# A gated cross-attention and mixture-of-experts block on one core: each batch's x loaded ahead into the rows that later hold its normalised x, scatters placed round the last norm, and the routing weights of all batches made in one go

## The chip, the core and the metric

The program runs on one core of a Trainium2 chip. The metric is the device time of one execution in microseconds (us). Before the change the median of 3 runs is 420.44 us (420.35 to 422.11). A difference under 0.5% (2.1 us) is about what a measurement of this kernel cannot tell from no change.

## The reference, cut to what matters

Eight batches (NB = 8) of 100 tokens (SQ = 100) with 512 features (H = 512), each with a context of 722 rows. First a cross-attention with one head whose output is tiled 16 times, with scores normalised along the keys before the softmax; then a mixture of 8 experts of which each token takes two.

```python
def _L0_xattn_ref(query, key, value, mask, Wq, bq, Wk, bk, Wv, bv, Wout, bout, seq_mask):
    q = query @ Wq + bq
    k = key @ Wk + bk
    v = value @ Wv + bv
    scores = jnp.einsum('bqd,bkd->bqk', q, k) / math.sqrt(HIDDEN)
    scores = _layer_norm_scores(scores)
    scores = scores + jnp.where(m, jnp.float32(-1e-32), jnp.float32(0.0))
    attn = jax.nn.softmax(scores, axis=-1)
    head = jnp.einsum('bqk,bkd->bqd', attn, v)
    attention = jnp.tile(head, (1, 1, NUM_HEADS))
    return attention @ Wout + bout

def _L0_ffn_ref(x, router_w, w13, w2):
    logits = jnp.einsum('bsh,eh->bse', x, router_w)
    probs = jax.nn.softmax(logits, axis=-1)
    weights, indices = jax.lax.top_k(probs, K)
    weights = weights / (weights.sum(axis=-1, keepdims=True) + 1e-06)
    h13 = jnp.einsum('bsh,ehi->bsei', x, w13)
    gate, up = jnp.split(h13, 2, axis=-1)
    h = jax.nn.silu(gate) * up
    y = jnp.einsum('bsei,eih->bseh', h, w2)
    y_sel = jnp.take_along_axis(y, indices[..., None], axis=2)
    return (y_sel * weights[..., None]).sum(axis=2)
x = x + jnp.tanh(g_xattn[0]) * _L0_xattn_ref(_layernorm(x, axis=-1), ctx_1024, ...)
x = x + jnp.tanh(g_ffn[0]) * _L0_ffn_ref(_layernorm(x, axis=-1), ...)
```

## The kernel before, in words

The program is written out by hand for each engine, with semaphores between them; no scheduler moves anything. It has two stages.

**Attention, in rounds.** Round i (from -1 to 7) works on several batches at once. PE (lines 413 to 432) projects batch i's context to keys and values (L319), turns the probabilities of batch i-1 (L330), makes the query of batch i+1 (L305), turns the values and makes the scores of batch i (L338, L344), makes the head of i-1 (L356), the ranks of i-2 (L363, L364) and the output rows of i-1 (L372). DVE (lines 840 to 864) takes in turn `choose(i-2)` (the two best experts of each token), `add_attention(i-2)` (x plus the attention, and the statistics of the second norm), `make_weights(i-3)`, `ln1_stats(i+2)` (statistics of the raw x), `fix_query(i+1)`, `make_values(i)`, `score_stats(i)`, `make_places(i-2)`, `set_pick(i-2)`, `raw_logits(i-1)`. POOL (lines 1033 to 1045) takes `count_taken(i-2)`, `norm2(i-2)`, `mark_sums(i)`, `norm1(i+2)`, `sigma(i)` (the factor and bias of the softmax of batch i, on which ACT's exponential L532 waits), and `scatter(i-3)`: two indirect DMAs (L1014) that write each token of a batch into the lists of its two experts in DRAM. ACT makes the exponentials, the copies out of PSUM, stores x plus attention to the output (`store_x2`, L561), and writes the normalised rows into `xn2[:, b, :]` (`normalise2`, L554), which it also puts into DRAM (L557). SP loads x, the transposed x and the context of the batches in their order, then the first expert's weights (L244, L281).

The raw x of batch b lies in `x_t[b % 6]`, a ring of six places of which two are the tiles yw and xg. `add_attention` writes its sum over it in place, so the load of batch 6 has to wait for the norm and the store of batch 0, and that of batch 7 for those of batch 1. These waits stand in SP's own order, ahead of everything that it loads later:

```python
                if b >= NX:
                    sp.wait_ge(S["xn2_ready"], b - NX + 1)
                    sp.wait_ge(S[f"out_put{b % NX}"], 16 * (b // NX))
                load_x(b)
```

**Between the stages.** After the last round PE picks the rows of the first tile by matmuls with `pick` (L380), which need the normalised rows of all batches; POOL works off what is left (`norm2` of batches 6 and 7 and the last scatters); DVE makes the tables of tiles. ACT copies the first tile's rows (`first_x_hi`, L634), DVE their low part (L943), and PE starts tile 0.

**Experts, in tiles of 128 list entries.** There are 16 tiles. Weights come as 1 MB pieces; ACT makes the high part of each piece (`split_hi`, L600, units 0 to 9 for one expert) and DVE the low part (`split_lo`, L819). For tile t PE does the gate and up products (L473), turns h (L480), turns the x rows of the next tile (`turn_x`, L460) and does the down products (L493); ACT makes silu (L644) and the scaled output rows (`y_out`, L660). In the last tile of each expert ACT and DVE also split the weights of the next expert. Behind `y_out` on ACT stand the split of units 8 and 9 and the next tile's silu. POOL runs a serial chain: `fetch(t+1)` (the piece of the list, L1080; the indices, L1082; the gather of the rows, L1086; the gather of the weights, L1092), `add_rows(t-1)` (the scatter-add into the output, L1106, whose landing it waits for), `entries_pass(t)` (L1101, for which `y_out(t)` waits). The loop is entered at `entries_stay(1)` (L1097). Ahead of it POOL waits for all scatters to land, starts the list of tile 0 (L1112), does `fetch(1)`, and gathers the weights of tile 0 (L1117). SP starts the next expert's loads (L289, L293; 6 MB) when the gather of `fetch(1)` has landed.

## Time and profile before

| what | us |
|---|---|
| median of 3 runs | 420.44 |
| the profiled execution, its own time | 422.71 |
| its span, first to last instruction | 421.1 |
| PE busy / DVE / ACT / POOL | 377.9 / 224.4 / 190.1 / 165.6 |
| mean granted clock of PE, as a share of 2.4 GHz | 0.952 |
| DMA: 77.75 MB | mean 185 GB/s |

The span is the time between the first and the last instruction of one profiled execution; the execution's own time is 1.6 us longer. Busy time adds up all instructions of an engine; an engine can be idle with no harm done. The places in the span are us from its start. In what follows T0 is the start of tile 0's first matmul.

### The profile page before, as it was taken

What the parts mean: (1) busy time and instruction counts of PE and PEld (TensorE: products, weight loads), DVE (VectorE), ACT (ScalarE), POOL (GpSimd) and SP (SyncE); (2) the same over time, 40 slices, a digit from 0 to 9 for tenths busy, and PEclk for the clock granted to TensorE, in tenths of its full rate; (3) what the DMA queues carried; (4) which work ended last, traced back from release to release, by engine and by line L of the source; (5) the groups of instructions that cost most, each with busy time, mean ns of one, the idle gap of its engine ahead of it and who ended that gap; (6) DMA issues with size and microseconds to landing.
All of it is one profiled execution on the core that took longest, in us unless ns stands there. A gap on an engine that the chain in (4) does not pass through costs nothing.

```text
span 421.1 us, 7238 instructions
## 1 busy us (share of the span) xinstructions
PE 377.9 (90%) x2046; PEld 288.2 (68%) x2047; DVE 224.4 (53%) x470; ACT 190.1 (45%) x314; POOL 165.6 (39%) x259
## 2 busy tenths in 40 slices
PE   1979994996868999998999999999999999999970
PEld 1435553475657887886888888888888888888850
DVE  2135883697930765387862239618644762973110
ACT  1123452464711862468642246528625643852220
POOL 2433574578941405515132241613434151451310
PEclk9979996899797999999999999999999999999995
DMA  7976799721208988197982228726762982210301
GB/s 253 372 258 199 273 326 352 292 80 48 33 5 309 418 341 246 28 313 271 371 307 42 50 48 291 237 102 186 262 232 33 324 252 82 50 27 4 50 0 16
DMA packets 18828, 77.75 MB, mean 185 GB/s; under 512 B 4957, under 2 KB 6109, under 8 KB 11647
## 3 DMA queue, kind: packets, MB, share of 16 engines
q1 hardware_dynamic: 11870, 66.80, 44.0%
q0 software_dynamic: 5184, 7.52, 9.5%
q10 hardware_dynamic: 1760, 3.28, 2.5%
q8 instruction: 6, 0.10, 0.1%
q14 instruction: 8, 0.06, 0.1%
HBM read 70.95 MB, written 7.55 MB: 186 GB/s over the span
## 4 chain that ended last, share of the span: by engine, by line
PE 66%; DMA 16%; POOL 6%; issue 6%; ACT 2%; DVE 1%; POOLq 1%; DVEq 0%; SPq 0%; ACTq 0%
PE scp L493 18%; PE turnB L473 17%; PE turnA L473 16%; PE kvp L319 4%; DMA x_t<-in_x_dram 3%; PE kvp L480 3%; DMA lists_d<-entry,place 3%; DMA ent_next<-lists_d 2%; DMA out_dram<-yw,ent 2%; DMA mask_u<-in_mask_dram 2%; POOL lists_d L1014 2%; PE scp L460 2%; DMA xg<-xn_d,gidx 1%; PE scp L344 1%; PE turnA L372 1%
## 5 line engine op out<-in xcount | busy, mean ns | idle before, releaser
L819 DVE TENSOR_TENSOR w13l<-stage,w13h 128x1024 fp32r<-128x1024 f32 x64 | 76.0, 1219 | 4.0 <-ACT w13h L600 3.4
L600 ACT ACTIVATE w13h<-stage 128x1024 fp32r<-128x1024 f32 x64 | 65.0, 1053 | 0.0
L473 PE MATMUL turnA<-w13h,xTh 128*128 128x512 f32 x128 | 51.8, 405 | 1.6 <-DVE xTl L943 1.6
L493 PE MATMUL scp<-w2h,hTh 128*128 128x512 f32 x128 | 52.2, 407 | 0.0
L473 PE MATMUL turnB<-w13h,xTh 128*128 128x512 f32 x128 | 52.0, 406 | 0.0
L473 PE MATMUL turnA<-w13h,xTl 128*128 128x512 f32 x128 | 51.4, 402 | 0.0
L473 PE MATMUL turnA<-w13l,xTh 128*128 128x512 f32 x128 | 51.4, 401 | 0.0
L473 PE MATMUL turnB<-w13l,xTh 128*128 128x512 f32 x128 | 50.9, 398 | 0.0
L493 PE MATMUL scp<-w2h,hTl 128*128 128x512 f32 x128 | 50.7, 396 | 0.0
L473 PE MATMUL turnB<-w13h,xTl 128*128 128x512 f32 x128 | 50.6, 395 | 0.0
L493 PE MATMUL scp<-w2l,hTh 128*128 128x512 f32 x128 | 50.5, 394 | 0.0
L819 DVE TENSOR_TENSOR w2l<-stage,w2h 128x2048 fp32r<-128x2048 f32 x16 | 35.9, 2288 | 21.3 <-ACT w2h L600 21.3
L913 DVE TENSOR_TENSOR h_t<-turnA,sg 128x256 f32<-128x256 f32 x32 | 12.8, 420 | 55.4 <-ACT sg L644 54.9
L1106 POOL DMA_INDIRECT out_dram<-yw,ent x16 | 29.8, 1862 | 15.8 <-ACT yw L660 11.3
L660 ACT ACTIVATE yw<-scp,ent 128x512 f32<-128x512 f32 x16 | 11.0, 687 | 51.1 <-PE scp L493 48.4
L644 ACT ACTIVATE sg<-turnB 128x256 f32<-128x256 f32 x32 | 12.3, 384 | 47.3 <-PE turnB L473 47.3
L1101 POOL COPY ent<-ent_now 128x3 int32<-128x3 int32 x15 | 4.8, 323 | 71.3 <-DMA out_dram<-yw,ent 71.3
L913 DVE TENSOR_TENSOR h_t<-turnB,sg 128x256 f32<-128x256 f32 x32 | 13.5, 422 | 34.0 <-ACT sg L644 29.4
L1014 POOL DMA_INDIRECT lists_d<-entry,place x16 | 27.9, 1744 | 6.1 <-issue 5.8
L473 PEld LDWEIGHTS turnA<-w13h,xTh 128*128 128x128 f32 x128 | 24.6, 192 | 7.7 <-issue 1.9
L917 DVE TENSOR_TENSOR hTl<-kvp,hTh 128x256 fp32r<-128x256 f32 x64 | 24.0, 416 | 10.9 <-ACT hTh L649 10.6
L600 ACT ACTIVATE w2h<-stage 128x2048 fp32r<-128x2048 f32 x16 | 29.7, 1904 | 0.0
(177 smaller groups left out, 654.3 us busy)
## 6 DMA issues: line engine op xcount, KB each, us to landing
stage<-in_w_dram SPq DMA_DIRECT2D x48, 1024.0 KB, 6.6
ctx_t<-in_ctx_dram SPq DMA_DIRECT2D x8, 1444.0 KB, 12.1
xT_t<-in_xT_dram SPq DMA_DIRECT2D x8, 200.0 KB, 8.2
xn_d<-xn ACTq DMA_DIRECT2D x8, 200.0 KB
x_t<-in_x_dram SPq DMA_DIRECT2D x6, 200.0 KB
out_dram<-x_t ACTq DMA_DIRECT2D x6, 200.0 KB
stage<-in_wout_dram SPq DMA_DIRECT2D x1, 1024.0 KB, 12.3
lists_d<-entry,place POOLq DMA_INDIRECT x16, 5.3
```

What stands on the lines that cost most here:

```text
L319: mm = pe.matmul(kvp[strip * D:(strip + 1) * D, 0:HK], sm[:, o:o + D], ctx_t[b % NC][:, c, half * HK:(half + 1) * HK], start=(c == 0), sto ...
L473: mm = pe.matmul(region, xp[:, c, :], wp[:, q, c, :], start=(c == 0 and i == 0), stop=(c == HC - 1 and i == 2))
L480: mm = pe.transpose(kvp[:, (q % 2) * 512 + j * P:(q % 2) * 512 + (j + 1) * P], h_t[:, q, j * P:(j + 1) * P], ident[:])
L493: mm = pe.matmul(scp[:, 512:512 + H], hp[:, q, j * P:(j + 1) * P], wp[:, q * QC + j, :], start=(q == 0 and j == 0 and i == 0), stop=(q == ...
L600: act.activation(dst, src, ACT.Copy).then_inc(S["w_hi"], 1)
L644: act.activation(sg[q % 2][:], region, ACT.Silu).then_inc(S["silu_done"], 1)
L660: act.activation(yw[:], scp[:, 512:512 + H], ACT.Copy, scale=ent[:, 2:3].bitcast(F32)).then_inc(S["y_ready"], 1)
L819: dve.tensor_tensor(lo, raw, hi.bitcast(F32), ALU.subtract).then_inc(S["w_lo"], 1)
L913: dve.tensor_tensor(h_t[:, q, :], region, sg[q % 2][:], ALU.mult).then_inc(S["h_done"], 1)
L917: dve.tensor_tensor(hTl[:, q, :], kvp[:, (q % 2) * 512:(q % 2) * 512 + QW], hTh[:, q, :].bitcast(F32), ALU.subtract).then_inc(S["hl_done"], 1)
L1014: pool.indirect_dma_start(lists_d, bass.IndirectOffsetOnAxis(place[:, b, k:k + 1], 0), entry[:, b, k, :], None).then_inc(S[f"lists_put{k}" ...
L1106: pool.indirect_dma_start(out_rows, bass.IndirectOffsetOnAxis(ent[:, 0:1], 0), yw[:], None, bounds_check=T - 1, oob_is_err=False, compute_ ...
```

## The change

It has five parts.

1. x of batch b is loaded into `xn2[:, b, :]`, the place of its normalised rows (eight places, so no load waits for a buffer). In SP's order the loads of x stand one batch earlier, and the waits for the norm, the store and `wx9_made` are gone. `add_attention` writes its sum into a ring `x2` of four (yw, xg and two more), and waits there for the store and the norm of batch b-4.
2. `scatter(b)` goes in round b+2, a round earlier. After the rounds POOL takes norm2(6), scatter(6), norm2(7), scatter(7); before, the scatters of batches 5, 6 and 7 were all still to do.
3. `make_weights` runs once for all eight batches, behind the low part of the first tile's x; `logit_exp` keeps its results by batch and no longer waits for it.
4. On DVE the low splits of units 0 and 1 stand in rounds 6 and 7, those of 2 and 3 after `add_attention(6)` (before: unit 0 in round 7, 1 and 2 after `add_attention(6)`, 3 after the tables). Ahead of unit 4 DVE waits for `lists_sent`, which POOL gives once its last scatter is issued.
5. POOL waits for the lists, the tables and the store, does `fetch(1)` first, and only then starts the list of tile 0.

```diff
-        NC, NX, NT = 3, 6, 3
+        NC, NX, NT, N2 = 3, NB, 3, 4
-        x_t = [sb(a, f"x_t{i}", [SQ, H])[:] for i in range(NX - 2)] + [yw[0:SQ, :], xg[0:SQ, :]]
+        x2 = [yw[0:SQ, :], xg[0:SQ, :]] + [sb(a, f"x2{i}", [SQ, H])[:] for i in range(N2 - 2)]
...
-                sp.dma_start(x_t[b % NX], x[b]).then_inc(S[f"x_in{b % NX}"], 16)
+                sp.dma_start(xn2[:, b, :], x[b]).then_inc(S[f"x_in{b % NX}"], 16)
...
+            load_x(3)
             load_ctx(2)
...
             for b in range(3, NB):
-                if b == 4:
-                    sp.wait_ge(S["wx9_made"], 1)
-                if b >= NX:
-                    sp.wait_ge(S["xn2_ready"], b - NX + 1)
-                    sp.wait_ge(S[f"out_put{b % NX}"], 16 * (b // NX))
-                load_x(b)
+                if b + 1 < NB:
+                    load_x(b + 1)
...
-            sp.wait_ge(S["weight_made"], NB)
+            sp.wait_ge(S["weight_made"], 1)
...
             def logit_exp(b):
                 act.wait_ge(S["nlmax_done"], b + 1)
-                if b >= 1:
-                    act.wait_ge(S["weight_made"], b)
...
             def add_attention(b):
                 dve.wait_ge(S["out_done"], b + 1)
-                dve.scalar_tensor_tensor(out=x_t[b % NX], in0=outp[0:SQ, :], scalar=gs[:, 0:1], in1=x_t[b % NX],
+                if b >= N2:
+                    dve.wait_ge(S[f"out_put{b % N2}"], 16 * (b // N2))
+                    dve.wait_ge(S["xn2_ready"], b - N2 + 1)
+                dve.scalar_tensor_tensor(out=x2[b % N2], in0=outp[0:SQ, :], scalar=gs[:, 0:1], in1=xn2[:, b, :],
...
-                if live(i - 3):
-                    make_weights(i - 3)
-                if i == NB - 1:
-                    split_lo(0, 0)
+                if i >= NB - 2:
+                    split_lo(0, i - NB + 2)
...
-            make_weights(NB - 3)
-            for unit in (1, 2):
+            for unit in (2, 3):
                 split_lo(0, unit)
...
-            make_weights(NB - 1)
+            make_weights()
+            dve.wait_ge(S["lists_sent"], 1)
             for unit in range(4, W_UNITS):
                 split_lo(0, unit)
...
-            for i in ROUNDS:
-                if live(i - 2) and i <= NB:
+            for i in range(-1, NB):
+                if live(i - 2):
                     count_taken(i - 2)
-                if live(i - 2):
                     norm2(i - 2)
...
-                if live(i - 3):
-                    scatter(i - 3)
+                if live(i - 2):
+                    scatter(i - 2)
...
-            for k in range(2):
-                pool.wait_ge(S[f"lists_put{k}"], 16 * NB)
+            count_taken(NB - 2)
+            norm2(NB - 2)
+            scatter(NB - 2)
+            norm2(NB - 1)
+            scatter(NB - 1)
+            pool.sem_inc(S["lists_sent"], 1)
...
+            for k in range(2):
+                pool.wait_ge(S[f"lists_put{k}"], 16 * NB)
+            pool.wait_ge(S["tiles_ready"], 1)
+            pool.wait_ge(S["out_put1"], 32)
+            fetch(1)
             pool.dma_start(ent[:, 0:2], lists_d[0:P, :]).then_inc(S["first_in"], 16)
-            pool.wait_ge(S["tiles_ready"], 1)
-            pool.wait_ge(S["out_put5"], 16)
-            fetch(1)
```

SP's order of loads round batches 5 to 7 (x_t, xT_t and ctx_t are x, the transposed x and the context of a batch; stage is a 1 MB piece of the first expert's weights), before:

```order
L235 DMA xg<-in_x_dram 100x512
L238 DMA xT_t<-in_xT_dram 128x400
L241 DMA ctx_t<-in_ctx_dram 128x2888
L244 DMA stage<-in_w_dram 128x2048
L235 DMA x_t<-in_x_dram 100x512
L238 DMA xT_t<-in_xT_dram 128x400
L241 DMA ctx_t<-in_ctx_dram 128x2888
L244 DMA stage<-in_w_dram 128x2048
L235 DMA x_t<-in_x_dram 100x512
L238 DMA xT_t<-in_xT_dram 128x400
L241 DMA ctx_t<-in_ctx_dram 128x2888
```

and in the changed kernel, the same stretch:

```order
L235 DMA xn<-in_x_dram 100x512
L238 DMA xT_t<-in_xT_dram 128x400
L241 DMA ctx_t<-in_ctx_dram 128x2888
L244 DMA stage<-in_w_dram 128x2048
L235 DMA xn<-in_x_dram 100x512
L238 DMA xT_t<-in_xT_dram 128x400
L241 DMA ctx_t<-in_ctx_dram 128x2888
L244 DMA stage<-in_w_dram 128x2048
L238 DMA xT_t<-in_xT_dram 128x400
L241 DMA ctx_t<-in_ctx_dram 128x2888
```

The x ahead of a batch's transposed x is now that of the next batch, so the last group has none, and x(7) stands ahead of batch 6's context instead of behind it.

POOL's order after the last softmax factor (L1002 before, L997 now), through the norms (L988 to L993; now L983 to L988) and the scatters (L1014; now L1009) to the fetch for tile 1, before:

```order
L1002 TENSOR_SCALAR sig<-lns,sig 100x1
L1014 DMA lists_d<-entry,place 7296x2 x2
L1007 TENSOR_TENSOR taken<-taken,both 100x8
...
L993 TENSOR_SCALAR rs<-ltop,rs 100x1
L1014 DMA lists_d<-entry,place 7296x2 x2
L988 TENSOR_SCALAR ve<-ln 100x1
...
L993 TENSOR_SCALAR rs<-ltop,rs 100x1
L1014 DMA lists_d<-entry,place 7296x2 x4
L1112 DMA ent<-lists_d 128x2
```

and now:

```order
L997 TENSOR_SCALAR sig<-lns,sig 100x1
L1009 DMA lists_d<-entry,place 7296x2 x2
L1002 TENSOR_TENSOR taken<-taken,both 100x8
...
L988 TENSOR_SCALAR rs<-ltop,rs 100x1
L1009 DMA lists_d<-entry,place 7296x2 x2
L983 TENSOR_SCALAR ve<-ln 100x1
...
L988 TENSOR_SCALAR rs<-ltop,rs 100x1
L1009 DMA lists_d<-entry,place 7296x2 x2
L1077 TENSOR_LOAD tile_row
```

Two scatters of the eight that followed the last factor have gone into the rounds, and the list of tile 0 (L1112) no longer stands ahead of the fetch.

## Rows read from the trace of the kernel before

**Rows 1.** Windows: us; busy of PE, PEld, DVE, ACT, POOL; clock, DMA share, GB/s.
```profile
52.48:59.80 7.32, 7.32 (x76) 4.11 (x75) 6.44 (x29) 3.93 (x8) 5.71 (x13) 1.00 0.99 359
59.80:74.64 14.84, 9.38 (x76) 5.17 (x75) 7.25 (x34) 6.02 (x12) 8.11 (x19) 0.75 0.99 332
74.64:83.27 8.63, 8.63 (x76) 4.41 (x75) 5.04 (x21) 3.74 (x7) 3.86 (x10) 0.84 0.79 289
91.33:107.11 15.78, 10.73 (x94) 8.85 (x92) 11.52 (x47) 9.20 (x15) 12.96 (x16) 0.92 0.20 53
134.35:152.40 18.05, 18.05 (x85) 14.76 (x84) 12.88 (x17) 11.74 (x18) 5.22 (x4) 1.00 1.02 402
```
**Rows 2.** Chain that ended last, in order of time: start, us, what.
```profile
54.42 14.53 DMA x_t<-in_x_dram
...
107.45 11.18 DMA lists_d<-entry,place
...
166.38 0.66 PE scp L460 x4
```
**Rows 3.** SP's timeline: a weight piece, x(6), context 7.
```profile
40.89 0.43 SPq L244 DMA_DIRECT2D stage<-in_w_dram  x1
...
51.51 0.31 SPq L235 DMA_DIRECT2D x_t<-in_x_dram  x1
...
55.17 0.43 SPq L241 DMA_DIRECT2D ctx_t<-in_ctx_dram  x1
```
**Rows 4.** PE's timeline, the two long stops.
```profile
70.42 1.27 PE L356 MATMUL turnA<-probT,vn 128*64 128x100 f32 x12 [5.41 <-DVE vn L738]
...
127.81 1.11 PE L460 MATMUL scp<-ident,xg 128*128 128x128 f32 x4 [4.99 <-DMA xg<-xn_d,gidx]
```
**Rows 5.** POOL's timeline, one round with scatters.
```profile
56.74 0.21 POOL L1007 TENSOR_TENSOR taken<-taken,both 100x8 f32<-100x8 f32 x1
...
58.75 0.23 POOL L979 TENSOR_SCALAR ve<-ln 100x1 f32<-100x1 f32 x1
...
61.18 0.27 POOL L1002 TENSOR_SCALAR sig<-lns,sig 100x1 f32<-100x1 f32 x1
...
64.41 0.21 POOL L1007 TENSOR_TENSOR taken<-taken,both 100x8 f32<-100x8 f32 x1
```
**Rows 6.** DVE's timeline, low splits ahead of and in tile 0.
```profile
93.15 2.35 DVE L819 TENSOR_TENSOR w13l<-stage,w13h 128x1024 fp32r<-128x1024 f32 x2
...
101.69 1.21 DVE L819 TENSOR_TENSOR w13l<-stage,w13h 128x1024 fp32r<-128x1024 f32 x1
...
107.56 4.62 DVE L819 TENSOR_TENSOR w13l<-stage,w13h 128x1024 fp32r<-128x1024 f32 x4
112.11 4.49 DVE L819 TENSOR_TENSOR w2l<-stage,w2h 128x2048 fp32r<-128x2048 f32 x2
```
**Rows 7.** POOL's timeline beside them, and into the expert stage.
```profile
93.28 3.08 POOL L1014 DMA_INDIRECT lists_d<-entry,place  x1 [0.30 <-issue]
...
101.93 1.11 POOL L991 TENSOR_SCALAR rs<-ln,rs 100x1 f32<-100x1 f32 x1
...
107.45 10.01 POOL L1014 DMA_INDIRECT lists_d<-entry,place  x1 [0.30 <-issue]
...
124.36 1.09 POOL L1086 DMA_INDIRECT xg<-xn_d,gidx  x1 [0.85 <-POOL gidx L1082]
...
127.01 0.95 POOL L1117 DMA_INDIRECT ent<-weights_d,ent  x1 [0.30 <-issue]
130.57 0.18 POOL L1097 COPY ent_now<-ent_next 128x3 int32<-128x3 int32 x1 [2.61 <-issue]
```
**Rows 8.** ACT's timeline, the high splits ahead of the last norm.
```profile
99.60 2.93 ACT L600 ACTIVATE w13h<-stage 128x1024 fp32r<-128x1024 f32 x3
```
**Rows 9.** Line L241, the eight loads of context: from issue to landing.
```profile
DMA to landing us min/median/max: 6.2/12.1/17.9
```
**Rows 10.** Line L1092, the sixteen gathers of weights: from issue to landing.
```profile
DMA to landing us min/median/max: 2.5/3.2/7.5
```

More of the change, by code:

```diff
@@ L160, in gated_block @@
         taken = sb(a, "taken", [SQ, NB + 1, E])
[L161 removed]
+        wgt = sb(a, "wgt", [SQ, 3, NB])
         hr = sb(a, "hr", [SQ, 2, E])
@@ L179, in gated_block @@
         xTl = sb(es, "xTl", [P, HC, P], F32R)
[L182 to L183 removed]
+        names = """x_in0 x_in1 x_in2 x_in3 x_in4 x_in5 x_in6 x_in7 xT_in0 xT_in1 xT_in2 ctx_in0 ctx_in1 ctx_in2 small_in wout_in bout_in mask_in
+        lists_set lists_put0 lists_put1 out_put0 out_put1 out_put2 out_put3 xn2_put weights_put lists_sent
         ident_made ones_made inv_made sel_made zero_made iotas_made empty_made mask_made emask_made tanh_done
@@ L553, in normalise2 @@
                 act.wait_ge(S["nmean2"], b + 1)
-                act.activation(xn2[:, b, :], x_t[b % NX], ACT.Identity, bias=rs2[b % 2][:, 1:2], scale=rs2[b % 2][:, 0:1]
+                act.activation(xn2[:, b, :], x2[b % N2], ACT.Identity, bias=rs2[b % 2][:, 1:2], scale=rs2[b % 2][:, 0:1]
                                ).then_inc(S["xn2_ready"], 1)
@@ L801, in set_pick, with make_weights @@
                                          op0=ALU.is_equal, op1=ALU.mult).then_inc(S["pick_set"], 1)
-            def make_weights(b):
-                dve.wait_ge(S["lexp_done"], b + 1)
-                dve.tensor_tensor(wgt[:, 0:1], e8[:, 0:1], e8[:, 1:2], ALU.add).then_inc(S["wgt_sum"], 1)
-                dve.wait_ge(S["wgt_sum"], b + 1)
-                dve.scalar_tensor_tensor(out=wgt[:, 1:2], in0=e8s[:], scalar=TOPK_EPS, in1=wgt[:, 0:1],
-                                         op0=ALU.mult, op1=ALU.add).then_inc(S["wgt_eps"], 1)
-                dve.wait_ge(S["wgt_eps"], b + 1)
-                dve.reciprocal(wgt[:, 2:3], wgt[:, 1:2]).then_inc(S["wgt_rec"], 1)
-                dve.wait_ge(S["wgt_rec"], b + 1)
-                dve.tensor_scalar(wt[:, b, :], e8[:, 0:2], wgt[:, 2:3], g_t[0:SQ, 1:2], ALU.mult, ALU.mult
-                                  ).then_inc(S["weight_made"], 1)
+            def make_weights():
+                dve.wait_ge(S["lexp_done"], NB)
+                dve.tensor_tensor(wgt[:, 0, :], e8[:, :, 0], e8[:, :, 1], ALU.add).then_inc(S["wgt_sum"], 1)
+                dve.wait_ge(S["wgt_sum"], 1)
+                dve.scalar_tensor_tensor(out=wgt[:, 1, :], in0=e8s[:], scalar=TOPK_EPS, in1=wgt[:, 0, :],
+                                         op0=ALU.mult, op1=ALU.add).then_inc(S["wgt_eps"], 1)
+                dve.wait_ge(S["wgt_eps"], 1)
+                dve.reciprocal(wgt[:, 2, :], wgt[:, 1, :]).then_inc(S["wgt_rec"], 1)
+                dve.wait_ge(S["wgt_rec"], 1)
+                dve.scalar_tensor_tensor(out=wt[:], in0=e8[:, :, 0:2], scalar=g_t[0:SQ, 1:2],
+                                         in1=wgt[:, 2, :].unsqueeze(2).to_broadcast([SQ, NB, 2]),
+                                         op0=ALU.mult, op1=ALU.mult).then_inc(S["weight_made"], 1)
             def split_lo(e, unit):
@@ L879, in _ @@
             dve.tensor_scalar(fill[:], steps_num[:], count, None, ALU.is_lt, ALU.add, accum_out=nt[:, 1:2]).then_inc(S["nt_ready"], 1)
-            make_weights(NB - 2)
             dve.wait_ge(S["nt_ready"], 1)
@@ L1119, in _ @@
             pool.sem_inc(S["ent_copied"], 1)
-            for j in range(NX):
-                pool.wait_ge(S[f"out_put{j}"], 16 * ((NB - 1 - j) // NX + 1))
+            for j in range(N2):
+                pool.wait_ge(S[f"out_put{j}"], 16 * NB // N2)
             n_tiles = pool.value_load(first_tile[0:1, E:E + 1], min_val=E, max_val=TILES - 1)
```

18 lines of the change are left out of this document (7 added, 11 removed).

## The prediction

> **What bounds the kernel now.** I read the windows by stage first, then the chain that ended last, then the timelines of PE, SP, POOL and DVE where the chain leaves PE. The reader is to see three things.
>
> First, a steady attention round takes 7.32 us with PE busy throughout, but the next two take 14.84 and 8.63 [rows 1], 8.8 us too much. In the first of them PE stands for 5.41 us at L356 behind DVE's values [rows 4], and DVE stands there because `ln1_stats(7)` is ahead in its order and x(7) has not landed: it is issued at 54.42 and lands 14.53 us later [rows 2]. It is late because SP was held before x(6) until 51.51 [rows 3] by the store of batch 0. The rest of the 8.8 is clock: 0.75 and 0.84 granted instead of 1.00 in these two windows [rows 1].
>
> Second, from the last softmax factor (91.33) to the first matmul of tile 0 (T0, 107.11) there are 15.78 us [rows 1].
>
> Third, the expert stage's first two tiles are bound by POOL's serial chain, not by PE. The chain goes from the last scatter (107.45, with its landing 11.18 us) through the fetches to the gather of x(3), which PE turns at 166.38 [rows 2]. From T0, a PE that never stood would be there after 15.5 us (its stop before 127.81 of 4.99 us begins at 122.8, somewhat over T0 + 15.5 [rows 4]) and two tiles of 18.05 [rows 1]: at T0 + 51.6 = 158.7. So 7.7 us of the end come from POOL's chain, and shortening PE's stop alone gives nothing. 
> *Loads of x ahead.* x(6) and x(7) now depend on no store. x(7) goes right behind the weight piece of 40.89 [rows 3], x(6) earlier; even at 17.9 us, the longest that a context takes [rows 9], it is there at 59.2, ahead of PE's stop, which begins at 65.0 (70.42 - 5.41 [rows 4]). The stop and its low clock go. Late next is POOL. Its own round with scatters takes 64.41 - 56.74 = 7.67 us [rows 5], above PE's 7.32, and the scatters now begin a round earlier. Before, sigma(4) is ready at 61.45; one POOL-bound round more makes that 61.8 (7.67 - 7.32). Another at 7.67 gives 69.5 for sigma(5). The next has no `norm1` (two of the six instructions from 58.75 to 61.45 [rows 5], 0.9 us of the 2.7), so 6.8 gives 76.3; the last is PE's again, 7.25: 83.5. The low splits of units 0 and 1 now stand in rounds 6 and 7. By where they fall, one misses POOL's reads narrowly and one holds a scatter for about half a microsecond, partly in slack: 0.2. sigma(7) is ready at 83.7 instead of 91.33: **-7.6**. Bounds: if each of the two splits holds POOL for its 1.2 us [rows 6] with some 0.4 for what follows, -4.5; if neither does, -7.8.
>
> *DVE's ring of four and the batched weights.* The store of b-4 is issued four rounds before its place is written, over 20 us; a landing is at most some 18 us in the fullest stretch. 28 small instructions of `make_weights` go, but DVE has idle time in every round, and the 0.85 us of the remaining run stands where one batch's stood. 0.
>
> *Context 7.* Issued at 55.17 [rows 3], it landed at worst 17.9 us later [rows 9], 73.1. PE will want it at 75.2 (59.80 and two rounds of 7.67) instead of 83.27. Less is queued ahead of it than before. 0, with 2 us of cover; if that is gone, each microsecond costs one.
>
> *The tail of the attention.* Two scatters less stand ahead of T0, but on T0's path it is these that count: the 3.08 us scatter (2.1 too long) meets its split otherwise; the split of unit 3 no longer stretches the last norm (0.84) but, waiting for ACT, meets norm2(6) and costs about 1.0. POOL would be ready 1.9 us sooner, but ACT's three high splits of 2.93 us [rows 8] end only 10.1 us behind sigma(7) (now 102.53, 11.2 behind; they follow norm2(6), which comes 1.1 sooner), and there the last normalisation then starts, instead of 11.7 behind, when L991 was done (103.04 [rows 7]): **-1.6**. Bounds 0 and -1.9. T0 becomes 83.7 + 14.2 = 97.9.
>
> *From T0 to POOL's loop.* Before, the loop begins at 130.57 [rows 7], T0 + 23.5. Now the scatters are issued by T0 - 0.9, ahead of the splits, so `lists_sent` holds DVE for nothing, and the lists land by T0 + 2.5. The list for tile 1 follows at T0 + 6. But its index instruction L1082 falls into the run of splits, which ends at T0 + 9.5 as before: the block moves from the scatter to the fetch. The gather is then issued at T0 + 10.4, lands 3.45 us later (127.81 - 124.36 [rows 4, 7]), ahead of PE's need at T0 + 15.5; the stop of 4.99 us goes. Behind the gather come the weights, and only now the list of tile 0, issued at 13.1, and its weights at 15.6. Before, L1117 at 127.01 stood 9.5 us behind the scatter's end; now it is 6.1 behind the end of the splits. But SP's 6 MB start when the gather lands, T0 + 14, and these two transfers run into them. A gather of weights takes 2.5 to 7.5 us to land [rows 10]; I take 5, between the median and the longest, as traffic is dense. With 1.3 us of register work the loop starts at T0 + 22: **-1.5** beside T0's own gain. Bounds: 2.5 us landings give T0 + 19.4 (-4.1); 7.5 and a late list T0 + 26.5 (+3.0).
>
> *From the loop to x(3).* 130.57 to 166.38 is 35.8 us of serial transfers in weight traffic; the same traffic follows the same engines, so I take the same 35.8. PE now reaches x(2) ahead of it and stops there for 3 to 4 us, a stop that before lay in tile 0; the clock falls behind such a stop (the window with a 5.41 us stop shows 0.75 [rows 1]). I add **+0.5**, for most of it is hidden in POOL's chain. Bounds 0 and 2. Tile 3 on is PE's and unchanged.
>
> Sum: -7.6 - 1.6 - 1.5 + 0.5 = **-10.2 us**. It is made against the profiled execution of 422.71 us, which would be 412.5; the median of the runs is 2.3 us lower, so 420.44 - 10.2 = **410.2**.
>
> **Rule against row.** The last scatter stood for the whole run of six splits, 10.01 us. The Trainium skill, page "SBUF — State Buffer", section "SBUF: two separate sides", holds that whichever of a DVE and a GpSimd operation starts first has the shared ports for that one instruction. By it the waiting read would get in at the next boundary of two splits, after 1.2 us at most; the trace disagrees before, but it is a rival here (below). The same page, section "Who interferes with whom", infers that a tensor_tensor on DVE does not stop descriptor generation on GpSimd; were that so, the 10.01 us would belong to the scatter, which is the slower rival.
>
> **Rivals.** *(a) The fetch gets in between the splits.* Its read could fall on a boundary where a split waits for ACT. Then the gather goes at T0 + 7 instead of 10.4 and everything behind it is 3 to 4 us earlier: 410.2 - 4 = 406. Against it the unbroken 10.01 us. 0.12.
>
> *(b) Context 7 takes the place of x(7).* DMA share is 0.99 already [rows 1], and the rounds want the data 8 us sooner. Landing 7 us after the need costs 5 net: 415. For it the 17.9 us; against it that it would need 24. 0.12.
>
> *(c) The first entries are late.* The list and weights of tile 0 land at the slow end, the loop starts at T0 + 26.5 and PE's stop in tile 1 grows: +4.5, 414.7, and with POOL held twice by the splits in the rounds (3 us) 417.7. 0.12.
>
> *(d) Slower: the long issue belongs to the scatters.* If it is the backlog of POOL's queue and not DVE's splits, the place of the block is open, and it can fall on scatter(6), which now stands ahead of norm2(7). Price: 9.0 us on T0 and, as DVE waits for `lists_sent`, another such issue of scatter(7), from T0 - 1.9 to T0 + 8.1, holds splits 4 to 9 by 7.5: 410.2 + 9.0 + 7.5 = 426.7. It decides once the block is over the 9.2 us of T0's gain. Against it: three long POOL instructions all end with DVE's splits, and one of them is no DMA. 0.03.
>
> *(e) Little is gained.* The rounds stay as they are because POOL, not x, sets them, and the fetch chain gives the rest back: within 2.1 us of 420.4. 7.67 against 14.84 speaks against it. 0.03.
>
> **How the numbers follow.** The forecast has 0.58, its own range by the bounds 406.5 to 414.5. To hold eight in ten I reach to (a), (b) and part of (c): 404.5 to 416.5. PE's floor for x(3), T0 + 51.6 = 149.5, is 6.4 us under POOL's chain (166.38 - 10.7 + 0.2 = 155.9), so nothing lies under 404. Faster by over 0.5% is the forecast, (a), (b) and most of (c): 0.94; same 0.03; slower 0.03.
>
> **What would show it.** Right: rounds of 7.3 to 7.7 us to the end and no stop at L356; sigma(7) near 84; T0 near 98; no scatter over 3 us; L1082 for tile 1 some 3 us long, ending with the sixth split; no PE stop before x(1), one of 3 to 4 us before x(2); L1097's first at T0 + 22. Wrong: a stop at the projection of batch 7, DVE idle before split 4, or an L1082 of 0.2 us.

## The result, and the profile after

The changed kernel takes **416.38 us** (median of 4 runs, 414.67 to 418.47) beside 421.27 us for the kernel before (4 runs, 420.35 to 423.28): ratio 0.989, 95% interval 0.984 to 0.994. It is faster, by 4.9 us, where 10.2 were forecast. Beside its own variants on two further chips there was no gain to be seen: 421.01 against 419.67 us (run e1, ratio 1.007 [1.002, 1.012]) and 418.52 against 419.49 us (run e10, 1.004 [0.999, 1.010]). So the 4.9 us hold for the first set of runs alone. The kernel before spreads over 412.6 to 428.0 us on the chips of the experiments (one run of 947.65 left aside), far more than the 2.1 us put down ahead for what cannot be told from no change. Each ratio is taken over the runs within 1.5% of the kernel's fastest, so it can differ from the quotient of the medians.

The profiled execution after takes 417.08 us (span 415.5), 5.6 less than the one before. Its windows by stage answer to [rows 1] (columns as there: us; busy of PE, PEld, DVE, ACT, POOL; granted clock, DMA share, GB/s):

```profile
59.89:67.56 7.67, 7.38 (x75) 4.13 (x74) 5.76 (x25) 4.89 (x9) 6.09 (x15) 1.00 1.01 341
67.56:75.22 7.66, 7.39 (x75) 4.13 (x74) 6.14 (x24) 4.88 (x9) 5.96 (x15) 1.00 1.00 328
75.22:83.55 8.33, 7.67 (x76) 4.62 (x76) 6.71 (x28) 5.06 (x10) 6.81 (x14) 1.00 0.66 217
83.55:100.10 16.55, 12.97 (x98) 10.90 (x96) 9.57 (x39) 9.36 (x15) 10.20 (x15) 0.79 0.28 84
100.10:115.13 15.03, 15.03 (x63) 12.11 (x63) 11.48 (x14) 7.32 (x12) 7.96 (x6) 0.89 0.12 25
115.13:138.05 22.92, 18.22 (x87) 14.68 (x85) 11.47 (x17) 11.41 (x19) 6.72 (x7) 0.99 1.00 402
138.05:158.19 20.14, 19.58 (x85) 15.81 (x85) 10.06 (x12) 8.48 (x13) 7.12 (x7) 0.93 0.67 217
...
176.29:198.02 21.73, 19.82 (x86) 15.87 (x85) 17.18 (x20) 15.03 (x21) 7.95 (x8) 0.92 0.84 302
198.02:216.80 18.78, 18.20 (x87) 14.70 (x85) 11.19 (x16) 9.14 (x15) 7.99 (x7) 1.00 0.80 289
```

The round of 14.84 us is gone; the rounds are 7.67 and 7.66, and the last softmax factor (sigma(7)) is ready at 83.55 instead of 91.33. But from there to T0 it now takes 16.55 us, not 15.78, at a clock of 0.79. And the tile from 176.29 to 198.02 takes 21.73 us.

SP's timeline shows x(7) and context 7, for [rows 3]:

```profile
40.85 0.37 SPq L235 DMA_DIRECT2D xn<-in_x_dram  x1
...
54.66 0.33 SPq L241 DMA_DIRECT2D ctx_t<-in_ctx_dram  x1
```

PE's timeline, the tail and the stops in the tiles, for [rows 4] (the last bracket is the idle time before the group and what ended it):

```profile
90.92 0.34 PE L360 MATMUL turnB<-both,tri 100*100 100x8 f32 x2 [1.30 <-issue]
...
91.54 2.45 PE L377 MATMUL kvp<-pick,xn 100*128 100x128 f32 x16
94.11 2.08 PE L377 MATMUL kvp<-pick,xn 100*128 100x128 f32 x8
96.27 2.08 PE L377 MATMUL kvp<-pick,xn 100*128 100x128 f32 x8
100.10 0.79 PE L470 MATMUL turnA<-w13h,xTh 128*128 128x512 f32 x1 [1.75 <-DVE xTl L937]
...
138.05 0.69 PE L457 MATMUL scp<-ident,xg 128*128 128x128 f32 x2 [4.70 <-DMA xg<-xn_d,gidx]
...
191.59 0.43 PE L477 MATMUL kvp<-ident,h_t 128*128 128x128 f32 x2 [1.91 <-DVE h_t L907]
```

DVE's timeline in the tail (splits of units 2 and 3, then the last batch's choice), which answers to [rows 6]:

```profile
85.02 1.19 DVE L818 TENSOR_TENSOR w13l<-stage,w13h 128x1024 fp32r<-128x1024 f32 x1
87.78 1.23 DVE L818 TENSOR_TENSOR w13l<-stage,w13h 128x1024 fp32r<-128x1024 f32 x1 [1.57 <-ACT w13h L595]
...
90.70 0.17 DVE L772 TENSOR_TENSOR both<-hot 100x8 f32<-100x8 f32 x1
```

Read the two together. Unit 3's low split stands 1.57 us for ScalarE's high split. Behind it on DVE wait the last batch's places, logits and `both`; PE needs `both` at L360 and stands 1.30 us (its row says issue, but `both` ends at 90.87 and PE starts at 90.92; the same stop in e13 below names it). The clock then falls, 16 picks run partly slow, and the two groups of eight take 2.08 us each at a granted clock of 0.50, where they take 1.16 at full clock. That is how T0 comes to 100.10.

POOL's timeline, for [rows 7]:

```profile
77.94 1.81 POOL L1009 DMA_INDIRECT lists_d<-entry,place  x1 [0.30 <-issue]
...
95.84 0.99 POOL L1009 DMA_INDIRECT lists_d<-entry,place  x1 [0.30 <-issue]
...
104.92 4.61 POOL L1080 TENSOR_SCALAR gidx<-ent_next 128x1 int32<-128x1 int32 x1 [3.55 <-DMA ent_next<-lists_d]
...
115.05 1.00 POOL L1117 DMA_INDIRECT ent<-weights_d,ent  x1 [1.70 <-DMA ent<-lists_d]
122.07 0.18 POOL L1095 COPY ent_now<-ent_next 128x3 int32<-128x3 int32 x1 [6.03 <-issue]
```

The 10.01 us scatter is gone. In its place the index instruction of tile 1 stands 4.61 us under DVE's splits (100.41 to 109.44), and POOL's loop starts at 122.07, T0 + 21.97. x(3) is turned at 158.19 instead of 166.38.

### The profile page after: what moved, and what is told of

It is laid out like the page before. It is cut to its first block, busy times and chain, and to the rows that moved or that the text cites. A ratio compares the mean times of both kernels' runs of the same rounds, so it can differ in the third digit from the quotient of the medians.

```text
span 415.5 us, 7206 instructions
## 1 busy us (share of the span) xinstructions
PE 376.4 (91%) x2046; PEld 288.1 (69%) x2047; DVE 220.7 (53%) x442; ACT 190.4 (46%) x314; POOL 164.2 (40%) x259
## 4 chain that ended last, share of the span: by engine, by line
PE 62%; DMA 18%; issue 7%; POOL 6%; DVE 2%; POOLq 2%; ACT 1%; DVEq 0%
PE scp L490 14%; PE turnB L470 14%; PE turnA L470 14%; DMA out_dram<-yw,ent 7%; PE kvp L316 6%; DMA ent_next<-lists_d 6%; PE turnA L302 2%; PE kvp L477 2%; DMA xg<-xn_d,gidx 2%; POOL gidx L1080 2%; PE turnA L369 2%; POOL ent_next L1090 1%; DMA ent<-weights_d,ent 1%; PE scp L457 1%; PE turnA L353 1%
## 5 line engine op out<-in xcount | busy, mean ns | idle before, releaser
L1104 POOL DMA_INDIRECT out_dram<-yw,ent x16 | 31.5, 1972 | 15.6 <-ACT yw L655 11.0
L1099 POOL COPY ent<-ent_now 128x3 int32<-128x3 int32 x15 | 6.8, 454 | 69.5 <-DMA out_dram<-yw,ent 69.5
L1084 POOL DMA_INDIRECT xg<-xn_d,gidx x16 | 25.1, 1571 | 13.4 <-POOL gidx L1080 13.4
```

The costliest lines, as they stand in the source:

```text
L1084: pool.indirect_dma_start(xg[:], None, xn2_d, bass.IndirectOffsetOnAxis(gidx[:], 0)).then_inc(S["gathered"], 16)
L1104: pool.indirect_dma_start(out_rows, bass.IndirectOffsetOnAxis(ent[:, 0:1], 0), yw[:], None, bounds_check=T - 1, oob_is_err=False, compute_ ...
```

## The experiments

16 runs of 12 kernels in five sets; the kernels of a set ran on one chip beside the kernel before. "Splits" are the low splits on DVE; "x ahead" is part 1 of the change.

| run | kernel | us, median (range) | before beside it | ratio, 95% interval |
|---|---|---|---|---|
| e1 | the whole change | 421.01 (419.72-422.30) | 419.67 | 1.007 [1.002, 1.012] |
| e2 | x ahead alone | 412.96 (408.46-417.41) | 419.67 | 0.979 [0.972, 0.986] |
| e3 | scatters, splits, fetch order; not x ahead | 418.65 (417.06-422.56) | 419.67 | 1.002 [0.997, 1.008] |
| e4 | whole, unit 3 late | 420.32 (419.08-422.50) | 419.67 | 1.006 [1.000, 1.011] |
| e5 | whole, units 0 to 3 at their old places | 412.58 (411.75-414.70) | 418.63 | 0.994 [0.990, 0.998] |
| e6 | whole, scatters at their old places | 419.89 (417.72-421.23) | 418.63 | 1.011 [1.003, 1.019] |
| e7 | e2, DVE holds back twice | 415.92 (414.16-419.17) | 418.63 | 1.001 [0.997, 1.006] |
| e8 | e2 again | 413.93 (408.12-418.72) | 418.63 | 0.983 [0.969, 0.997] |
| e9 | e5 again | 414.30 (412.37-416.05) | 419.49 | 0.994 [0.990, 0.998] |
| e10 | the whole change | 418.52 (415.53-422.08) | 419.49 | 1.004 [0.999, 1.010] |
| e11 | e5, list of tile 0 first | 409.30 (407.85-410.40) | 419.49 | 0.983 [0.977, 0.989] |
| e12 | e11, DVE waits for the index | 411.11 (409.48-413.89) | 419.49 | 0.988 [0.982, 0.995] |
| e13 | e5, unit 3 early | 417.67 (414.42-419.58) | 422.18 | 0.988 [0.984, 0.992] |
| e14 | e5, unit 0 in round 6 | 413.43 (412.95-414.14) | 422.18 | 0.980 [0.977, 0.983] |
| e15 | e14, list of tile 0 first | 408.27 (405.57-409.67) | 422.60 | 0.965 [0.960, 0.970] |
| e16 | e11 again | 410.03 (407.18-412.09) | 422.60 | 0.967 [0.961, 0.973] |

### e1 to e4: which part carries the gain

e1 is the kernel after, unchanged. e2 is the kernel before with every line of part 1 of the diff (`x_t` gone, `x2` a ring of four, x loaded into `xn2` a batch ahead), nothing else. e3 is the kernel before with parts 2, 4 and 5 alone, and its weights batch by batch. e4 is the whole change with

```diff
-            for unit in (2, 3):
-                split_lo(0, unit)
+            split_lo(0, 2)
...
                                      op0=ALU.mult, op1=ALU.add).then_inc(S["tiles_ready"], 1)
+            split_lo(0, 3)
```

> The changed kernel once more, as the measure for the others on this chip. Theory A (the lost microseconds sit at fixed places: T0 at 100.1 with the picks at the low clock, and one to two more behind a stop in tile 4): 414.5 to 417, T0 again at 100.1 with a granted clock of 0.5 between 94 and T0. Theory B (it was an unlucky draw of clock in one execution): T0 nearer 98 and the median under 413.

> Before plus part 1 alone (x loaded ahead, ring of four for the sums); scatters, splits, weights and the order of the fetch as before. Theory A (the load ahead is nearly all of the gain): the stop at L356 goes, sigma(7) at about 83, T0 = sigma(7) + 15.8 = 99, POOL's loop at T0 + 23.5 = 122.5, x(3) at 158.5, time as the whole change or within 1 us of it, 415 to 417. Rival (the scatters and the fetch carry half of it): 418 to 419.5.

> The change without part 1 and without the batched weights: x in the ring of six with SP's waits, scatters a round earlier, split positions, lists_sent and the fetch first as in the change. Theory A: the stop of some 5.4 us at L356 stays; the last scatter's issue is 1 us, L1080's index instruction is held for 4 to 5 us instead; T0 near 107, POOL's loop 1.5 us earlier than before, 419 to 421. Rival (the fetch order alone is worth its 4.99 us stop in tile 0): under 417.

> The changed kernel with one move: the low split of unit 3 again behind the tables of tiles, as before the change. Theory A (its new place makes DVE wait for ACT, so the ranks of batch 7 come late, PE stands 1.3 us, and the clock falls for the picks up to T0): DVE's wait of 1.6 us and PE's of 1.3 shrink to 0.7 or less, the clock from 91 to T0 is 1.0 up to the last norm, T0 at 98, and 2 us less than the changed kernel, 414. Rival (the picks run slow because they are few and small, wherever the split is): T0 stays at 100, no difference.

x ahead alone takes 412.96 us, 8 less than the whole change on the same chip. The rest of the change without it is worth nothing that could be told (418.65 against 419.67). So part 1 carries the whole gain and the other parts together give half of it or more back. Neither theory of e1 came out: 421.01 us lies above both ranges, with T0 at 104.09. e2 beat both of its ranges.

e3's forecast missed a thing that bears on the size of part 1. The stop at L356 was to stay at 5.4 us. In e3's profile it is 2.44 us (PE starts again at 59.72), and sigma(7) is ready at 87.71, where the one profile of the kernel before has 91.33. How long that stop is in other executions of the kernel before is not known, for it was profiled once. In this set sigma(7) is ready at 82.33 in e2, at 85.85 in e1 and at 87.71 in e3: with the other parts beside it, x ahead brings it 1.9 us forward here (e1 against e3).

Moving unit 3 alone (e4) did not bring the tail back: T0 was 104.44, beside 104.09 in e1. Both profiles have another fault, a stop of PE at L327 of 1.99 us, which the first profile of the change did not have. It is best seen in e10, the whole change on a third chip.

### e5, e6, e9, e10: splits or scatters

e5 and e9 are one kernel: scatters early, but the splits where they were before the change.

```diff
-                if i >= NB - 2:
-                    split_lo(0, i - NB + 2)
+                if i == NB - 1:
+                    split_lo(0, 0)
...
-            for unit in (2, 3):
+            for unit in (1, 2):
                 split_lo(0, unit)
...
+            split_lo(0, 3)
```

e6 keeps the splits of the change and puts the scatters back:

```diff
-                if live(i - 2):
-                    scatter(i - 2)
+                if live(i - 3):
+                    scatter(i - 3)
...
             norm2(NB - 2)
+            scatter(NB - 3)
+            norm2(NB - 1)
             scatter(NB - 2)
-            norm2(NB - 1)
             scatter(NB - 1)
```

> The whole change, but the low splits on VectorE stand where the kernel before has them (unit 0 in round 7, 1 and 2 behind add_attention(6), 3 behind the tables); the scatters stay a round early. Theory S (it is the splits in rounds 6 and 7, falling on POOL's reads, that make the tail late and low in clock): T0 is 97.5 to 99 instead of 100.1 to 104.1, no PE stop over 1 us after 80 us, time 411 to 414. Rival Q (it is POOL's queue with the scatters a round early, one pair more in front of each sigma): the rounds keep 7.7 to 7.9 us, T0 stays at 100 or later, 416 to 421.

> The whole change, but each scatter a round later again, as before the change; the splits stay in rounds 6 and 7. Theory S: T0 is late (100 to 104) as in the whole change, time 416 to 421, and some POOL instruction under a split takes 1 us more than its normal time. Rival Q: T0 98 to 99, rounds of 7.3 to 7.5 us, time 411 to 414.

> The whole change with the low splits at the places of the kernel before, once more, as the partner of the three others on this chip. Theory S: 411 to 415 again, T0 97.5 to 99.5, turns of x(2) and x(3) at T0+37 and T0+57, and 3 us or more under the whole change beside it.

> The whole change, a third time, beside its variants. Theory S: 415.5 to 421.5, T0 100 to 104, and its median at least 3 us over that of the variant with the splits at their old places; in its rounds 6 and 7 at least one POOL instruction is 1 us over its normal time under a split. If it comes out within 1 us of the variant, the placing of the splits is not what cost the gain.

The splits' places cost it. With them put back the kernel takes 412.58 and 414.30 us, 4.2 us under the whole change on the same chip (e9, e10); with the scatters put back instead it stays at 419.89. T0 is 98.35 and 97.30 in e5 and e9, 101.95 in e6, 100.30 in e10.

How they cost it: POOL's timeline of e10, a scatter in round 6, one in round 7, the last instruction of sigma(7),

```profile
69.11 2.20 POOL L1009 DMA_INDIRECT lists_d<-entry,place  x1 [0.52 <-issue]
...
76.91 2.12 POOL L1009 DMA_INDIRECT lists_d<-entry,place  x1 [0.53 <-issue]
...
83.83 1.36 POOL L997 TENSOR_SCALAR sig<-lns,sig 100x1 f32<-100x1 f32 x1
```

DVE's timeline of e10, the splits of units 0, 1, 2 and 3,

```profile
69.13 1.19 DVE L818 TENSOR_TENSOR w13l<-stage,w13h 128x1024 fp32r<-128x1024 f32 x1
...
76.85 1.19 DVE L818 TENSOR_TENSOR w13l<-stage,w13h 128x1024 fp32r<-128x1024 f32 x1
...
83.95 1.19 DVE L818 TENSOR_TENSOR w13l<-stage,w13h 128x1024 fp32r<-128x1024 f32 x1
...
88.65 1.23 DVE L818 TENSOR_TENSOR w13l<-stage,w13h 128x1024 fp32r<-128x1024 f32 x1 [3.51 <-ACT w13h L595]
```

and PE's timeline of e10:

```profile
86.23 0.73 PE L327 MATMUL turnB<-ident,prob 100*128 100x100 f32 x6 [1.99 <-ACT prob L529]
...
92.42 3.64 PE L377 MATMUL kvp<-pick,xn 100*128 100x128 f32 x16
```

Units 0 and 1 each begin together with a scatter, which takes 1.0 to 1.1 us over its normal 1.11. POOL bounds these rounds, so it stays late, and its last instruction of sigma(7) now meets unit 2's split and takes 1.36 us instead of 0.27. So sigma(7) is ready at 85.19 instead of 83.55, ScalarE's softmax is late, PE stands 1.99 us, and after that the 16 picks take 3.64 us (granted clock 0.53) where they took 2.05 in e5. In the first profile of the change the splits of units 0 and 1 began 0.6 and 1.2 us behind the first scatter of their round (70.04 against 69.47, 77.69 against 76.51), and held only the second, by 0.2 and 0.8 us: no stop. So it hangs on a fraction of a microsecond whether this placing stops PE at L327, and e1, e4, e6 and e10 all fell on the bad side, each with a stop of 1.99.

What the bad side costs is less regular. This table has, for each profile, when sigma(7) was ready, T0, the time between and the granted clock over it:

| run | unit 3 ahead | stop at L327 | sigma(7) | T0 | between | clock |
|---|---|---|---|---|---|---|
| after | yes | no | 83.55 | 100.10 | 16.55 | 0.79 |
| e13 (below) | yes | no | 85.29 | 101.81 | 16.52 | 0.96 |
| e10 | yes | yes | 85.19 | 100.30 | 15.11 | 0.89 |
| e6 | yes | yes | 85.29 | 101.95 | 16.66 | 0.69 |
| e1 | yes | yes | 85.85 | 104.09 | 18.24 | 0.54 |
| e4 | no | yes | 85.83 | 104.44 | 18.61 | 0.52 |
| e9 | no | no | 83.06 | 97.30 | 14.24 | 0.96 |
| e5 | no | no | 84.08 | 98.35 | 14.27 | 1.00 |
| e14 (below) | no | no | 83.33 | 97.58 | 14.25 | 1.00 |

e10 reaches T0 only 0.2 us behind the first profile, which was on the good side. e1 is the same kernel with the same stop and needs 3.1 us more than e10 behind sigma(7), at a clock of 0.54. What decides the clock there no run isolates, so the stop is shown and a fixed price for it is not. Of the 3.0 us by which e10's T0 lies behind e9's, 2.1 are ahead of sigma(7) and 0.9 behind it.

### e13, e14: which split

e13 puts unit 3 back to its place in the change, behind 1 and 2 (`for unit in (1, 2, 3)`, and none behind the tables); e14 puts unit 0 back into round 6 (`if i == NB - 2`).

> The scatters a round early, unit 0 in round 7 as before the change, and units 1, 2 and 3 together behind add_attention(6). If the split of unit 3 ahead of the last batch's values (where it waits for ScalarE, 3.5 us in the whole change) is what makes the tail late: T0 100 or later, DVE stands over 1.5 us before a split at 87 to 90, 416 to 419. If it is the split in round 6 and its twin in round 7 alone: no PE stop near 86, T0 98 to 99.5, 412 to 415.

> The scatters a round early, unit 0 in round 6 as in the whole change, units 1 and 2 behind add_attention(6) and 3 behind the tables as before the change. If the split in round 6 is enough to put POOL late: a scatter of 2.1 us near 69, sigma(7) ready at 84.5 to 85.5, a PE stop of 1 to 2 us near 86 and T0 at 99.5 to 104, 415 to 420. If it takes both splits (round 6 and round 7): sigma(7) ready at 83.5 to 84, T0 98 to 99, 412 to 415.

Unit 0 in round 6 alone did no harm: sigma(7) at 83.33, T0 at 97.58, 413.43 us. But its split began 0.56 us behind the scatter (69.77 against 69.21; 0.53 in e15), the good side of the first profile, so no run shows what it does alone on the bad side. With unit 3 early the kernel takes 4.2 us more (417.67), with no stop at L327 at all; the two also differ in unit 0's round. DVE's and PE's timelines of e13:

```profile
90.95 1.23 DVE L818 TENSOR_TENSOR w13l<-stage,w13h 128x1024 fp32r<-128x1024 f32 x1 [1.63 <-ACT w13h L595]
```
```profile
94.09 0.34 PE L360 MATMUL turnB<-both,tri 100*100 100x8 f32 x2 [1.30 <-DVE both L772]
```

It is the pattern of the first profile again: 1.6 us on DVE, 1.30 on PE. From sigma(7) to T0 it takes 16.52 us here and 16.55 in the first profile; without unit 3 ahead 14.27 (e5), 14.24 (e9), 14.25 (e14). So unit 3's place is 2.3 us of the tail where PE does not stop at L327. In e13 all of it lies ahead of L360 (8.80 us behind sigma(7), 6.52 in e14), with the picks at 1.16 us a group and a granted clock of 1.00 from L360 to T0. In the first profile 0.85 lies there (7.37) and the rest in the low clock behind it (0.72 from L360 to T0). So the two equal sums are made of unlike parts, behind stops of the same 1.30 us, and their agreement to 0.03 us is partly luck. e10, with unit 3 ahead too but sigma(7) held back by POOL, has 0.9 instead of 2.3.

In the profiles, e13's T0 is 4.2 us behind e14's: 2.3 behind sigma(7) and 2.0 ahead of it, for it is ready at 85.29 (the projection at 60.98, near no split, takes 3.54 us instead of 2.64). Why the latter, was not isolated. Behind T0, e13 needs 2.6 us less to x(3) and 2.5 more in two later tiles.

There are thus two faults in the placing, and either one shows: e4, which heals unit 3, keeps units 0 and 1 in two rounds; e13, which heals those, keeps unit 3.

### e7, e8, e11, e12, e15, e16: the chain behind T0

e7 is e2 with two waits on DVE and `fetch(1)` ahead of the list of tile 0:

```diff
+            dve.wait_ge(S["lists_sent"], 1)
             for unit in range(4, W_UNITS):
+                if unit == 2 * NQ:
+                    dve.wait_ge(S["first_fetch"], 1)
                 split_lo(0, unit)
```

(`first_fetch` is given by POOL when `fetch(1)` is issued.) e8 is e2 again. e11 is e5 with

```diff
+            pool.dma_start(ent[:, 0:2], lists_d[0:P, :]).then_inc(S["first_in"], 16)
             pool.wait_ge(S["tiles_ready"], 1)
             pool.wait_ge(S["out_put1"], 32)
             fetch(1)
-            pool.dma_start(ent[:, 0:2], lists_d[0:P, :]).then_inc(S["first_in"], 16)
```

e12 is e11 with a wait for `gidx_made` ahead of unit 8; e15 is e14 with the same early list; e16 is e11 again.

> The kernel before with the loads of x ahead alone, and VectorE made to leave POOL alone twice: it begins low split 4 only when the last scatter is issued, and unit 8 only when fetch(1) is issued; fetch(1) stands ahead of the list of tile 0. If the serial chain of POOL is held by VectorE's run of splits and sets x(1) to x(3): no scatter over 1.2 us, gather of x(1) issued near T0+8 instead of T0+16.5, the stop before x(1) under 1 us, POOL's loop at T0+17 to T0+19 instead of T0+22.6, x(3) near 154 instead of 158, time 3 to 4 us under the loads of x alone: 407 to 410. Rival: tile 0 pays for the later products of VectorE (4 us) and the chain's later transfers are slow in the weight traffic; no gain, 411 to 414.

> The loads of x ahead alone, once more, beside the others on one chip. It fell into two groups before (408.5 to 410.3 and 415.6 to 417.4). If the groups are small offsets that a run falls into, both come again, median 410 to 416; if the first was an accident of that chip, one group remains. In a profile of the faster group the stops of PE in tiles 1 to 5 should be shorter than the 7.5 us in all of the slower one, with x(3) at 152 to 155 instead of 158.2.

> The variant with the splits at their old places, and the list of tile 0 read ahead of fetch(1) instead of behind it. If it is the late entries of tile 0 that hold POOL's loop (6.3 us idle before the loop behind the weights of tile 0, issued at 112.9): those weights are issued 2.2 us sooner, right behind the gather of tile 1's weights, the loop starts at T0+19 to T0+20 instead of T0+21.8, the stop of PE before x(2) is 1.5 to 2.5 instead of 3.9, time 1 to 2.5 us under the partner. Rival: a landing in the weight traffic takes its time whenever it is issued; the loop stays at T0+21.5, no difference over 0.5 us.

> As the one before, and VectorE begins unit 8 only when the index of tile 1 is computed. If the run of six splits is what holds the index instruction (2.50 us against 0.25): it takes 0.3 us, gather of x(1) at T0+8 instead of T0+9.9, loop at T0+17 to T0+18, stop before x(2) under 1 us, but units 8 and 9 end 2 to 3 us later and PE stops 1 to 2.5 us in tile 0: x(2) turned within 1 us of the kernel without the gap, time 0 to 2 us under it. Rival: the lists land late (5 to 7 us behind the last scatter, as in the variant with the fetch gap), DVE stands over 4 us, time 2 to 4 us over it.

> The two best pieces together: unit 0 in round 6, units 1 and 2 behind add_attention(6), 3 behind the tables, scatters early, and the list of tile 0 read ahead of fetch(1). T0 97 to 98.5, POOL's loop at T0+16 to T0+17, no stop or one under 1 us before x(2), 407 to 410.5, and within 1 us of the variant with unit 0 in round 7 beside it. Rival: the two gains overlap (a later x(2) was only waited for in another place) and it stays at 412 or more.

> The fastest variant so far, once more on this chip: 407.5 to 411, 8 to 11 us under the kernel before. If its 409.3 was that chip's accident: 412 to 415, as the variants without the early list.

**Holding DVE back does not pay.** In e7 the scatter is free, but tile 0 paid, as the rival said (its 411 to 414 us were still too low): the list could only be read 6.3 us behind the last scatter, DVE stood 5.69 us and PE 4.43 us in tile 0. POOL's, DVE's and PE's timelines of e7:

```profile
106.56 0.62 POOL L1084 DMA_DIRECT2D ent_next<-lists_d  x1 [6.34 <-issue]
```
```profile
110.23 4.49 DVE L819 TENSOR_TENSOR w2l<-stage,w2h 128x2048 fp32r<-128x2048 f32 x2 [5.69 <-POOLq L1119]
```
```profile
115.11 1.09 PE L477 MATMUL kvp<-ident,h_t 128*128 128x128 f32 x4 [4.43 <-DVE h_t L913]
```

PE needed no data at x(1) and x(2), and x(3) was turned at 158.28, where e2 had 158.24: a stop moved from one tile to another. e12's smaller wait freed the index instruction (0.25 us) as expected, but brought none of the 0 to 2 us: the loop starts at T0 + 19.3, and the kernel takes 1.8 us more than e11, with ranges that overlap.

**The early list pays, by more than I had put down.** e11 takes 409.30 us, 5.0 under its partner e9; 1 to 2.5 were expected. POOL's timeline of e5, the weights of tile 0 and the loop,

```profile
112.89 1.00 POOL L1118 DMA_INDIRECT ent<-weights_d,ent  x1 [1.69 <-DMA ent<-lists_d]
120.19 0.18 POOL L1096 COPY ent_now<-ent_next 128x3 int32<-128x3 int32 x1 [6.30 <-issue]
```

and of e11:

```profile
109.18 0.95 POOL L1118 DMA_INDIRECT ent<-weights_d,ent  x1 [0.30 <-issue]
112.80 0.18 POOL L1096 COPY ent_now<-ent_next 128x3 int32<-128x3 int32 x1 [2.67 <-issue]
```

and SP's timeline of e11, the first of the next expert's weight pieces:

```profile
110.15 2.34 SPq L286 DMA_DIRECT2D stage<-in_w_dram  x4
```

SP starts its six pieces when the gather of x(1) lands. In e11 the small gather of weights is issued 1.0 us ahead of them and POOL goes on after 2.67 us; in e5 it is issued 0.9 us behind them (112.89 against 112.00) and takes 6.30. The other profiles fall in with it:

| run | gather issued, against SP's first piece | idle until the loop |
|---|---|---|
| e2 | 117.67, 118.84 | 2.49 |
| e15 | 109.16, 110.16 | 2.63 |
| e12 | 110.41, 110.69 | 5.51 |
| after | 115.05, 114.14 | 6.03 |

In these profiles a lead of 0.3 us is not enough and one of 1.0 is. The rest agree: all with a lead of 0.97 to 1.47 us (the kernel before, e8 and e16 too) wait 2.5 to 2.7 us, all with less or none 5.5 to 6.3. The loop of e11 starts at T0 + 15.98 instead of T0 + 21.8, and the stop before x(2) is gone (112.83 to 130.86, 18.03 us).

e15 and e16 beat the kernel before again, at 408.27 and 410.03 us, 14.3 and 12.6 under it (the whole change did not run beside them). They are 1.8 us apart (under 1 was expected) and overlap in their ranges and intervals, so no choice between them is shown; unit 0 in round 6 did no harm there either.

e8 did not settle the spread of x ahead alone: eight runs from 408.12 to 418.72, now without a gap between two groups. The two profiles, of e2 and e8, are of runs in the upper half (417.41 and 415.44), so what the shorter ones do differently stays open. This spread is also why e2 and e8 cannot be ranked against e5.

## Why the prediction was right in direction and half wrong in size

*Loads of x ahead, -7.6.* Right in the first profile: sigma(7) at 83.55, forecast 83.7; rounds of 7.67 and 7.66. The runs confirm that it carries the gain (e2, e3). The size leans on one profile of the kernel before, with its stop of 5.41 us at L356; e3, with the loads of x as before, has a stop of 2.44 and sigma(7) at 87.71, so what x ahead is worth differs from run to run. But the 0.2 us put down for the splits of units 0 and 1 in rounds 6 and 7 holds for one alignment only. In e1 and e10 sigma(7) was ready at 85.85 and 85.19. The step's own bound ("if each of the two splits holds POOL") was the case in four of the five profiles with x ahead and both splits there, and the text priced only POOL's time; the PE stop of 1.99 us and the low clock behind it were not in it.

*Ring of four, batched weights, context 7, 0.* Right: no wait at any of them; PE starts batch 7's projection at 75.22 with no stop.

*The tail, -1.6.* **This is the step that failed**, and the one whose cause the runs show; a second miss of the same size, in the tiles, is told below. T0 was forecast at sigma(7) + 14.2 and came at sigma(7) + 16.55. The text saw that unit 3's split would wait for ACT, and priced what it does to POOL's norm2(6), about 1.0 us off the path. It left out what is queued behind the waiting split on its own engine: the last batch's places, choice and `both`. That is 2.3 us (e13 against e5, e9, e14), and the sign of the term turns: +0.8 instead of -1.6. The 14.2 itself is right for the change with unit 3 behind the tables and no stop at L327: seven profiles have 14.12 to 14.44. With the stop, e4 has 18.61.

*From T0 to POOL's loop, T0 + 22.* Right: T0 + 21.97, with the block moved to the fetch's index instruction (4.61 us; about 3 forecast), no stop before x(1), and 6.0 us for the late weights of tile 0. What "run into them" meant was right, and e11 shows its price: 5 us of the whole kernel.

*From the loop to x(3), 35.8 + 0.5.* Right: 36.12, with a stop of 4.70 us before x(2) (3 to 4 forecast). The text is not of one piece here: its sum adds 0.5, its place of x(3) (155.9) only 0.2.

*"Tile 3 on is PE's and unchanged".* Wrong by 2.4 us. From x(3) to x(6) it is 58.61 us, before 56.25 (222.63 - 166.38). 1.79 of it is one tile: PE stands for DVE's h_t in both kernels (1.91 and 1.67 us), but the granted clock behind the stop is 0.61 after and 1.00 before. 0.58 is a late gather. That the clock falls there is not tied to the change by any run: one and the same kernel took 20.19 us in e11 and 21.71 in e16 for this tile. Still, all three profiles of the change have the slow tile (21.70 to 21.73), against e13 and e16 alone of its ten variants' profiles (20.19 to 20.24 in the other eight) and none of the kernel before, e2, e3, e7 and e8 (19.94 to 19.97). The cause stays open. These windows are from e16 and e11:

```profile
185.91:192.31 6.40, 6.40 (x25) 5.20 (x26) 5.42 (x8) 3.63 (x6) 0.00 (x0) 0.73 0.98 356
```
```profile
184.18:189.06 4.88, 4.88 (x24) 3.96 (x25) 4.88 (x8) 3.65 (x6) 0.00 (x0) 1.00 1.01 343
```

The sum against the profiled execution: forecast 412.5, measured 417.08. Of the 4.6 us, 2.2 are T0, -0.2 the way from there to x(3), 2.4 the three tiles behind it and 0.2 what follows. So no more than half of the miss is the failed step; the other half lies in the tiles, mostly in a clock that no run explains.

*The rivals.* (a) the fetch between the splits, (b) context 7 and (d) the scatter's own backlog did not come: the index instruction stood to the end of the run of splits, x and context were on time, and from 54 us on the scatters that met no split took 0.98 to 1.12 us. (c) was half there: POOL held twice by splits is what e1 and e10 show, with T0 at 104.09 and 100.30. Two of three profiles of the change have it; the text gave it a part of 0.12 and was too sure. Its other half, late entries with the loop at T0 + 26.5, did not come (T0 + 22.2 in both). (e), little gained, is what e1 and e10 measured (ratios 1.007 and 1.004), but not for its reason, since the long round was gone in both.

## What to carry to other kernels

When an instruction that may wait is moved ahead on an in-order engine, price the wait for what is queued behind it on that engine, not only for its effect on its neighbours; here filler work ahead of the last batch's short serial values cost 2.3 us. Keep long VectorE instructions such as these splits out of rounds that GpSimd bounds, or accept that a few tenths of a microsecond decide whether they stop the matmuls (splits that began together with a scatter did, those that began 0.6 us or more behind it did not). And a small gather on a serial chain belongs ahead of the big loads that its own predecessor sets off: one line moved was worth 5 us, as much as the whole change on its best chip.
